# Causal attention stage: transposes and projections on half tiles of the array, in two phases per pair of row tiles

## The chip, the cores and the metric

The program runs on one core of one Trainium2 chip. A core has five engines with programs of their own: TensorE (PE, matmuls and transposes; its weight loads have rows of their own, PEld), VectorE (DVE), ScalarE (ACT), GpSimd (POOL) and SyncE (SP, which issues transfers here). They wait for each other by semaphores. The metric is the time of one execution in microseconds on the device, as a median of runs.

## The reference

Four layers, each an attention and a feed-forward part, on x of 2 x 1024 x 128 in float32. The change touches the attention of layer 2 alone, a causal one with 16 heads of 64:

```
latent_kv = x @ w_kv_down
kv = latent_kv @ w_kv_up
k, v = (kv[..., :HD], kv[..., HD:])
q = (x @ w_q).reshape(Bx, Tx, N_HEAD, HEAD_SIZE)
att = jnp.einsum('bqhd,bkhd->bhqk', q, k) * scale
att = jnp.where(causal, att, -jnp.inf)
att = jax.nn.softmax(att, axis=-1)
y = jnp.einsum('bhqk,bkhd->bqhd', att, v)
return y @ w_out
```

## The kernel before

`causal_stage` computes q, k, v, the scores, the softmax and the product with v, all in float32. Rows of the sequence are cut into 8 tiles of 128 for each of 2 batches, and heads go two at a time (`hp`, 8 steps), since two heads of 64 fill 128 partitions. Under the causal mask row tile `tb` has `tb + 1` blocks of 128 keys. The stage goes over 64 pairs `n`: 8 steps x 2 batches x 4 pairs, where a pair is a short row tile (j = 0 to 3, so 1 to 4 blocks) and a long one (7 - j, so 8 to 5 blocks). A pair always has 9 blocks for each of two heads.

The steps of a row tile are these. `score` multiplies q and k: K is 64 partitions, so the two heads stand in the upper and the lower 64 rows of the array, as tiles of 64 rows x 128 columns (the profile prints 64*128). DVE (`maximum`, L1887) adds the mask, writes the negated scores to `p` and keeps their minimum. ACT (`exponential`, L1838) takes the exponential in place and sums the row. `turn` (L1766) transposes each 128 x 128 block of `p` on PE against the identity, a 128*128 operation, up to four blocks into one PSUM bank. ACT or DVE copies that bank to `pT` (`move`, L1829 and L1876). `product` (L1780) multiplies v and `pT`; its weights are the 64 columns of one head of v, so the two heads stand in the left and the right half of the array, as tiles of 128 rows x 64 columns (128*64). At the end of a batch `take` (L1844) copies the sums from PSUM to `y`, `invert` (L1895) inverts the row sums on DVE, SP carries them through memory to all partitions, and POOL (L1924) multiplies `y` by them. `project` makes a piece of the next step's q or k (L1732, one matmul of 512 columns, 128*128) or v (L1737, four of 128 columns, 128*128); a step needs 12 pieces, and they are spread 2, 1, 2, 1 over the pairs. The last step has none.

A float32 matmul shows as two MATMUL and two LDWEIGHTS records, a transpose as one of each.

PE's order of one pair is: long scores, short transposes, product of the previous long tile, pieces, next short scores, long transposes of head 0, short product, long transposes of head 1. Transposes and pieces share PSUM banks 4 and 5 in turn (`groups`, `number`, `bank_of`). Each group has one mover, ACT or DVE, and `open_bank` lets PE write group g when group g - 2 has been copied. `settled` waits for the copies that a product or a score reads. Scores use banks 0 to 3, a head two of them, and wait until DVE has read the scores before (`max_done`).

The stage behind this one (`out_stage`, L1329) multiplies `y` by the output weights; its second half needs the last batch's `y` from POOL.

Of the kernel before, what the change touches and what calls it, by code (L numbers as in the profile page):

```python
# [1601 lines left out]
def causal_stage(nc, R, ctx, W, dram, lat, y):  # L1602
# [27 lines left out]
    PIECES = 12  # L1630
    PER_STEP = 8
# [10 lines left out]
    def parts_of(n):  # L1642
        return range(row_tile(n, 1) // 4 + 1)


    def short_turns(n):
        return [("turn", n, 0, (0, 1), 0)] if row_tile(n, 0) < 2 else [("turn", n, 0, (hh,), 0) for hh in range(2)]

    def long_turns(n, hh):
        return [("turn", n, 1, (hh,), part) for part in parts_of(n)]  # L1650

# [3 lines left out]

    def pieces(n):
        hp, j = n // PER_STEP, n % PER_STEP
        if hp + 1 == STEPS:
            return []
        first = 3 * (j // 2) + 2 * (j % 2)  # L1660
        return [(hp + 1, m) for m in range(first, first + (1 if j % 2 else 2))]


    groups = [(("project", 0, m), "da"[m % 2]) for m in range(PIECES)]
    for n in range(PAIRS):
        groups += [(x, "da"[i]) for i, x in enumerate(short_turns(n))]
        groups += [(("project", *x), "da"[i]) for i, x in enumerate(pieces(n))]
        groups += [(x, "ad"[i]) for i, x in enumerate(long_turns(n, 0))]
        groups += [(x, "da"[i]) for i, x in enumerate(long_turns(n, 1))]
    number = {what: g for g, (what, _m) in enumerate(groups)}  # L1670
    moved_by_a, moved_by_d = [0], [0]
    for _what, mover in groups:
        moved_by_a.append(moved_by_a[-1] + (mover == "a"))
        moved_by_d.append(moved_by_d[-1] + (mover == "d"))

    def bank_of(what):
        return 4 + number[what] % 2

# [34 lines left out]
    def on_pe(pe):  # L1713
        def settled(g):
            pe.wait_ge(t_a, moved_by_a[g + 1])
            pe.wait_ge(t_d, moved_by_d[g + 1])

        def open_bank(what):
            g = number[what]
            if g >= 2 and groups[g - 2][1] == "a":  # L1720
                pe.wait_ge(t_a, moved_by_a[g - 1])
            if g >= 2 and groups[g - 2][1] == "d":
                pe.wait_ge(t_d, moved_by_d[g - 1])
            return bank_of(what)

        def project(hp, m):
# [3 lines left out]
            if m < 8:  # L1730
                b, t = chunk(m % 4)
                pe.matmul(R.ps[:, bank, :], w[:, hp % 2, m // 4, :], h_chunk(R, m) if m < 4 else lat[:, b, t],  # L1732
# [8 lines left out]
        def score(n, long):  # L1741
# [8 lines left out]
            for c in range(end + 1):  # L1750
                cols = min(CW, full - c * CW)
                for hh in range(2):
# [3 lines left out]
                    if c == end:  # L1756
                        last.then_inc(s_full, 1)
# [904 lines left out]
```

## Time and profile before

| | us |
|---|---|
| median of 3 runs | 2167.46 |
| lowest and highest of them | 2165.61 and 2169.25 |
| the profiled execution's span, first to last instruction | 2163.0 |
| of it the causal stage, from its first piece to the last product | 562.4 |
| PE busy in the whole span | 2051.7 (95%) |
| DVE, ACT busy in the whole span | 1578.5, 1377.2 |

The page gives busy times by engine, a chain of work that ended last, and groups of instructions. A PE record lasts longer than its share of the array, because matmuls are pipelined: the distance from one stretch of equal instructions to the next tells what a stretch costs. "Idle before" is the time in which the engine had nothing running, with what ended it.

### The profile page before, as it was taken

To read this page: it belongs to the slowest core of one execution; us is meant where nothing else is said; L and a number is where in the kernel's file an instruction comes from. 1 tells how busy PE (TensorE), PEld (TensorE's weight loads), DVE (VectorE), ACT (ScalarE), POOL (GpSimd) and SP (SyncE) were. 2 spreads that over 40 slices of the span, in tenths; PEclk is the share of its full clock that TensorE was granted. 3 is DMA by queue.
4 is the path that set the end of the run, shared out by engine and by line. 5 is a ranking of instruction groups with operands and counts; after the bars stand their busy time and mean duration, and the time that the engine had idled before them with its cause. 6 is when DMAs were issued, how large, how long until landed. Compare 5 with 4: busy or idle time off the path is not lost. (4 is left out here: it accounts for less than half of the span.)

```text
span 2163.0 us, 40432 instructions
## 1 busy us (share of the span) xinstructions
PE 2051.7 (95%) x15666; PEld 901.1 (42%) x15666; DVE 1578.5 (73%) x2235; ACT 1377.2 (64%) x2731; POOL 208.9 (10%) x388
## 2 busy tenths in 40 slices
PE   7999999999999899999989999999999989999998
PEld 3222222222223422222336666666666434444453
DVE  7999999999984799999466565566655355555553
ACT  4899999999995389899755555555555322222253
POOL 3010111111023301111000000000000100000000
PEclk7999999999999799999999999999999999999999
DMA  3010100001000100110100111011101145554520
GB/s 97 4 26 15 32 21 24 21 25 28 15 25 10 40 22 22 27 38 12 29 5 11 22 17 25 11 25 15 21 11 22 26 95 119 128 122 115 121 60 20
DMA packets 107005, 82.44 MB, mean 38 GB/s; under 512 B 54720, under 2 KB 89536, under 8 KB 102864
## 3 DMA queue, kind: packets, MB, share of 16 engines
q1 hardware_dynamic: 105872, 79.05, 16.0%
q8 instruction: 120, 1.97, 0.4%
q10 hardware_dynamic: 432, 0.56, 0.1%
q0 software_dynamic: 528, 0.43, 0.1%
q14 instruction: 53, 0.43, 0.1%
HBM read 62.98 MB, written 2.42 MB: 30 GB/s over the span
## 5 line engine op out<-in xcount | busy, mean ns | idle before, releaser
L1069 DVE TENSOR_REDUCE a0nm<-ps 128x2 f32<-128x1024 f32 x512 | 586.4, 1213 | 10.4 <-PE ps L936 8.2
L1047 ACT ACTIVATE a0p<-ps 128x512 f32<-128x512 f32 x1024 | 544.2, 599 | 60.2 <-PE ps L956 43.5
L970 PE MATMUL ps<-a0p,a0vst 128*32 128x256 f32 x4096 | 328.0, 392 | 27.6 <-ACT a0p L1047 14.0
L1069 DVE TENSOR_REDUCE a1nm<-ps 128x2 f32<-128x1024 f32 x256 | 294.7, 1214 | 8.2 <-PE ps L936 7.3
L1047 ACT ACTIVATE a1p<-ps 128x512 f32<-128x512 f32 x512 | 275.6, 596 | 34.9 <-PE ps L956 26.0
L956 PE MATMUL ps<-a0qm,a0k 32*128 32x512 bf16 x1024 | 276.7, 387 | 0.0
L2120 ACT ACTIVATE ex_s<-ps 128x512 f32<-128x512 f32 x128 | 76.4, 597 | 252.9 <-PE ps L2075 252.9
L936 PE MATMUL ps<-a0k,a0q 32*128 32x512 bf16 x1024 | 202.9, 394 | 18.0 <-DVE a0nm L1069 15.8
L1887 DVE CUSTOM_DVE_ANT_0 cap_long<-ps,xc_res 128x1024 f32<-128x1024 f32 (+3 forms) x128 | 126.0, 1022 | 76.5 <-PE ps L1754 76.5
L1838 ACT ACTIVATE cap_long<-cap_long,canm 128x1024 f32<-128x1024 f32 (+3 forms) x128 | 125.3, 982 | 81.9 <-DVE canm L1887 81.9
L2209 DVE TENSOR_TENSOR ex_su<-ex_s,ps 128x512 f32<-128x512 f32 x128 | 88.1, 688 | 113.7 <-PE ps L2079 113.0
L970 PE MATMUL ps<-a1p,a1vst 128*32 128x256 f32 x2048 | 164.3, 393 | 6.4 <-ACT a1p L1047 5.5
L956 PEld LDWEIGHTS ps<-a0qm,a0k 32*128 32x128 bf16 x1024 | 79.2, 91 | 208.4 <-ACT a0p L1047 118.2
L1754 PE MATMUL ps<-cak,caq 64*128 64x512 f32 (+3 forms) x768 | 158.6, 517 | 2.3 <-DVE canm L1887 2.3
L936 PE MATMUL ps<-a1k,a1q 64*128 64x512 bf16 x512 | 149.9, 401 | 10.9 <-DMA a1q<-a1parts_sb 5.9
L956 PE MATMUL ps<-a1qm,a1k 64*128 64x512 bf16 x512 | 156.6, 386 | 0.0
L970 PEld LDWEIGHTS ps<-a0p,a0vst 128*32 128x32 f32 x4096 | 81.5, 108 | 155.8 <-ACT a0p L1047 70.7
L2075 PE MATMUL ps<-h_res,f2wg 128*128 128x512 f32 x256 | 130.7, 592 | 0.0
L2079 PE MATMUL ps<-h_res,f2wu 128*128 128x512 f32 x256 | 130.7, 592 | 0.0
L2063 PE MATMUL ps<-ex_hid,f2wd 128*128 128x512 f32 x256 | 130.5, 592 | 0.0
L1766 PE MATMUL ps<-ident_res,cap_long 128*128 128x128 f32 x832 | 122.4, 283 | 1.7 <-ACT capT_long L1829 0.9
L2220 DVE TENSOR_TENSOR ex_hid<-ex_su,ex_wb 128x512 f32<-128x512 f32 x128 | 88.6, 692 | 44.6 <-DMA ex_wb<-ex_w_dram 38.6
(324 smaller groups left out, 2531.6 us busy)
## 6 DMA issues: line engine op xcount, KB each, us to landing
ex_wb<-ex_w_dram SPq DMA_DIRECT2D x62, 512.0 KB, 6.2
carrow<-car_dram SPq DMA_DIRECT2D x32, 256.0 KB, 4.3
xc_res<-a0rec SPq DMA_DIRECT2D x15, 256.0 KB
a0q<-a0parts_sb SPq DMA_DIRECT2D x95, 32.0 KB, 2.0
a1q<-a1parts_sb SPq DMA_DIRECT2D x94, 32.0 KB
a0k<-a0parts_sb SPq DMA_DIRECT2D x90, 32.0 KB, 2.0
a1k<-a1parts_sb SPq DMA_DIRECT2D x84, 32.0 KB
f2wg<-in_ex_gate SPq DMA_DIRECT2D x32, 64.0 KB, 1.8
```

Source lines behind the costliest of these rows:

```text
L936: pe.matmul(R.ps[:, bank + d, :], q[rows, slot, rt, t0:t0 + 128], k[rows, slot, rt, hf * CW:(hf + 1) * CW], start=True, stop=True).then_in ...
L956: pe.matmul(R.ps[:, score_bank(n), :], k[rows, place(u)[3], rt, s * 128:(s + 1) * 128], qm[rows, u % 2, rt, :], start=True, stop=True).the ...
L970: last = pe.matmul(R.ps[32 * j:32 * j + 32, 6, cols], vst[:, g, s, j * HG // 4, :], p[:, s % 2, j, cols], start=(g == 0 and s == 0 and hal ...
L1047: act.activation(p[:, s % 2, e, :], R.ps[:, score_bank(n), :], ACT.Exp).then_inc(exp_done, 1)
L1069: dve.tensor_reduce(nm[:, u % 2, tb, 2 - 2 * z:4 - 2 * z, hf], R.ps[:, bank:bank + 2, :], X_AXIS, ALU.max, negate=True).then_inc(bank_free, 1)
L1754: last = pe.matmul(R.ps[:, 2 * hh + c, 0:cols], q[rows, hp % 2, b, tb * 128:(tb + 1) * 128], k[rows, hp % 2, b, c * CW:c * CW + cols], sta ...
L1766: last = pe.transpose(R.ps[:, bank, to:to + 128], p[long][:, hh, s * 128:(s + 1) * 128], R.ident[:])
L1838: act.activation(row, row, ACT.Exp, bias=nm[:, a % 4:a % 4 + 1], scale=-1.0, accum_out=rs[:, b, tb, hh:hh + 1]).then_inc(exp_done, 1)
L1887: dve.tensor_tensor_reduce(p[long][:, hh, 0:(tb + 1) * 128], src, late[:, T - (tb + 1) * 128:T], -1.0, LARGEST, ALU.add, ALU.min, nm[:, a ...
L2063: pe.matmul(R.ps[:, i % 4, :], wd[:, (i // 4) % 2, :], hid[:, i % 4, :], start=False, stop=True, skip_group_check=True).then_inc(d_done, 1)
L2075: pe.matmul(R.ps[:, G_BANK + 2 * (i % 2), :], wg[:, slot, :], h_chunk(R, c), start=True, stop=True)\
L2079: pe.matmul(R.ps[:, U_BANK + 2 * (i % 2), :], wu[:, slot, :], h_chunk(R, c), start=True, stop=True)\
```

## The change

Transposes: a 128 x 128 block of `p` is turned as two tiles, partitions 0 to 63 and 64 to 127, each 64 rows x 128 columns of the array with 64 moving columns. The upper rows go to one PSUM bank, the lower rows to the next one, so a `turn` now fills both banks 4 and 5; ACT copies the even group, DVE the odd one, each half of the columns. Eight blocks of a head fit in one turn (8 x 64 columns), so a long head is one turn of two groups, where it was two parts of up to four blocks.

Projections: each matmul is issued as two of 64 columns of the array (128*64), the left and the right half of the output's partitions, as the products are.

Order on PE: scores and transposes (all 64*128) come in one phase, products and pieces (all 128*64) in the other. The short scores of the next pair and the first bank of the next long scores are issued between the long transposes of this pair; short scores move to bank 1 or 3. The pieces are now two per pair for six pairs and none for two. ACT and DVE orders follow: exponentials and maxima are taken one head at a time, and `invert` stands behind the last copy of the batch.

```diff
+    HALVES = (slice(0, PH), slice(PH, 2 * PH))
...
+    def turns(n, heads, long):
+        return [("turn", n, long, heads, half) for half in range(2)]
...
+        if hp + 1 == STEPS or j >= PIECES // 2:
             return []
+        return [(hp + 1, 2 * j + i) for i in range(2)]
...
+        def open_bank(what):
+            g = number[what]
+            if g >= 2:
+                pe.wait_ge(t_d if g % 2 else t_a, moved(g - 2))
             return bank_of(what)
...
-                pe.matmul(R.ps[:, bank, :], w[:, hp % 2, m // 4, :], h_chunk(R, m) if m < 4 else lat[:, b, t],
-                          start=True, stop=True).then_inc(t_full, 1)
+                for cols in HALVES:
+                    last = pe.matmul(R.ps[cols, bank, :], w[:, hp % 2, m // 4, cols], h_chunk(R, m) if m < 4 else lat[:, b, t],
+                                     start=True, stop=True)
+                last.then_inc(t_full, 1)
...
+        def turn(pair):
+            _t, n, long, heads, _half = pair[0]
+            banks = [open_bank(what) for what in pair]
             pe.wait_ge(exp_done, scores_of(n, long) + heads[-1] + 1)
+            blocks = [(hh, s) for hh in heads for s in range(row_tile(n, long) + 1)]
+            for i, (hh, s) in enumerate(blocks):
+                for bank, rows in zip(banks, HALVES):
+                    last = pe.transpose(R.ps[:, bank, i * PH:(i + 1) * PH], p[long][rows, hh, s * 128:(s + 1) * 128],
+                                        R.ident[rows, rows])
+                    if i + 1 == len(blocks):
+                        last.then_inc(t_full, 1)
...
         for n in range(PAIRS):
-            score(n, 1)
-            for x in short_turns(n):
-                turn(x)
-            if n:
-                product(n - 1, 1)
-            for x in pieces(n):
-                project(*x)
             if n + 1 < PAIRS:
-                score(n + 1, 0)
-            for x in long_turns(n, 0):
-                turn(x)
-            product(n, 0)
-            for x in long_turns(n, 1):
-                turn(x)
-        product(PAIRS - 1, 1)
+                short_score(n + 1)
+            turn(long_turns(n, 0))
+            if n + 1 < PAIRS:
+                long_score_first(n + 1)
+            turn(long_turns(n, 1))
+            if n + 1 < PAIRS:
+                long_score_rest(n + 1)
+                turn(short_turns(n + 1))
+            product(n, 1)
+            if n + 1 < PAIRS:
+                for x in pieces(n + 1):
+                    project(*x)
+                product(n + 1, 0)
...
     def on_act(act):
...
         for n in range(PAIRS):
+            move(long_turns(n, 0)[0])
             if n + 1 < PAIRS:
+                exponential(n + 1, 0, 0)
+                exponential(n + 1, 0, 1)
+            move(long_turns(n, 1)[0])
+            if n + 1 < PAIRS:
+                move(short_turns(n + 1)[0])
+                exponential(n + 1, 1, 0)
+            if ends_batch(n):
+                take(n)
+            if n + 1 < PAIRS:
+                exponential(n + 1, 1, 1)
+                for x in pieces(n + 1)[0:1]:
+                    move(("project", *x))
...
     def on_dve(dve):
...
         for n in range(PAIRS):
             if n + 1 < PAIRS:
+                maximum(n + 1, 0, 0)
+            move(long_turns(n, 0)[1])
+            if n + 1 < PAIRS:
+                maximum(n + 1, 0, 1)
+            move(long_turns(n, 1)[1])
             if ends_batch(n):
                 invert(n)
+            if n + 1 < PAIRS:
+                maximum(n + 1, 1, 0)
+                move(short_turns(n + 1)[1])
+                maximum(n + 1, 1, 1)
+                for x in pieces(n + 1)[1:2]:
+                    move(("project", *x))
```

PE's queue before, from the long scores of the second pair of a batch (row tiles 1 and 6) to those of the next. Line L1754 are scores, L1766 transposes, L1780 products, L1737 pieces of v; `cap` is p, `capT` is pT, `cav` is v, and x counts matmuls of the program:

```order
L1754 MATMUL ps<-cak,caq 128x512 x2
L1754 MATMUL ps<-cak,caq 128x384 x2
L1766 MATMUL ps<-ident_res,cap_short 128x128 x4
L1780 MATMUL ps<-capT_long,cav 64x128 x16
L1737 MATMUL ps<-a2qkv,sq_res 128x128 x4
L1754 MATMUL ps<-cak,caq 128x384 x2
L1766 MATMUL ps<-ident_res,cap_long 128x128 x7
L1780 MATMUL ps<-capT_short,cav 64x128 x4
L1766 MATMUL ps<-ident_res,cap_long 128x128 x7
L1754 MATMUL ps<-cak,caq 128x512 x2
```

PE's queue in the changed kernel over the same work, from the short scores of row tile 1 to the short product of that pair (L1750 scores, L1777 transposes, L1792 products, L1741 pieces of v):

```order
L1750 MATMUL ps<-cak,caq 128x256 x2
L1777 MATMUL ps<-ident_res,cap_long 128x64 x16
L1750 MATMUL ps<-cak,caq 128x512 x2
L1777 MATMUL ps<-ident_res,cap_long 128x64 x16
L1750 MATMUL ps<-cak,caq 128x384 x2
L1777 MATMUL ps<-ident_res,cap_short 128x64 x8
L1792 MATMUL ps<-capT_long,cav 64x128 x16
L1741 MATMUL ps<-a2qkv,sq_res 64x128 x16
L1792 MATMUL ps<-capT_short,cav 64x128 x4
```

The shape of the tile changed at every row before; now the first six rows have one shape and the last three the other.

ACT's queue before, around the end of a batch: exponentials are L1838, copies of transposes L1829, the copy of the sums to y L1844, copies of pieces L1827:

```order
L1838 ACTIVATE cap_long,cars<-cap_long,canm 128x1024 x2
L1844 ACTIVATE y<-ps 128x512 x2
L1827 ACTIVATE cak<-ps 128x512
L1829 ACTIVATE capT_long<-ps 128x512
L1838 ACTIVATE cap_short,cars<-cap_short,canm 128x256 x2
L1829 ACTIVATE capT_long<-ps 128x512
```

ACT's queue in the changed kernel at the same place and through the pair behind it (exponentials L1852, copies of transposes L1844, the copy to y L1858, pieces L1842):

```order
L1852 ACTIVATE cap_long,cars<-cap_long,canm 128x1024
L1858 ACTIVATE y<-ps 128x512 x2
L1852 ACTIVATE cap_long,cars<-cap_long,canm 128x1024
L1842 ACTIVATE cav<-ps 128x512
L1844 ACTIVATE capT_long<-ps 128x8x64
L1852 ACTIVATE cap_short,cars<-cap_short,canm 128x256 x2
L1844 ACTIVATE capT_long<-ps 128x8x64
L1844 ACTIVATE capT_short<-ps 128x2x2x64
```

The copy to y now stands between the two long exponentials, and the copy of the second long head stands behind both short exponentials with the copy of the short transposes next to it.

## Rows read from the trace of the kernel before

**Rows 1.** The page: the chain that ended last, by engine, shares of the span.

```profile
PE 42%; ACT 3%; DVE 2%; issue 1%; DMA 1%; POOL 0%; POOLq 0%; SPq 0%; DVEq 0%
```

**Rows 2.** Windows: us, busy PE, PEld, DVE, ACT, POOL; clock, DMA share, GB/s.

```profile
1113.46:1675.86 562.40, 554.12 (x4609) 359.68 (x4609) 333.51 (x782) 312.54 (x736) 38.48 (x31) 1.00 0.11 18
200.00:600.00 400.00, 367.99 (x4140) 115.18 (x4136) 394.53 (x382) 365.00 (x710) 44.91 (x129) 1.00 0.09 23
```

**Rows 3.** Timeline of PE over one pair: start us, length us, engine, line.

```profile
1413.54 0.44 PE L1780 MATMUL ps<-capT_short,cav 128*64 128x128 f32 x4
1413.91 1.14 PE L1766 MATMUL ps<-ident_res,cap_long 128*128 128x128 f32 x8
1414.98 1.77 PE L1754 MATMUL ps<-cak,caq 64*128 64x512 f32 x8
1416.68 0.66 PE L1766 MATMUL ps<-ident_res,cap_short 128*128 128x128 f32 x4
1417.27 1.97 PE L1780 MATMUL ps<-capT_long,cav 128*64 128x128 f32 x32
1419.17 1.12 PE L1732 MATMUL ps<-h_res,a2qkv 128*128 128x512 f32 x2
1420.22 0.92 PE L1754 MATMUL ps<-cak,caq 64*128 64x384 f32 x4
1421.07 0.98 PE L1766 MATMUL ps<-ident_res,cap_long 128*128 128x128 f32 x7
1421.98 0.33 PE L1780 MATMUL ps<-capT_short,cav 128*64 128x128 f32 x2
```

**Rows 4.** The chain in order of time: start us, us, one piece of v.

```profile
1175.52 1.09 PE ps L1737 x8
```

**Rows 5.** Timeline of the experts' matmuls: lines change, the tile does not.

```profile
1800.83 1.02 PE L2063 MATMUL ps<-ex_hid,f2wd 128*128 128x512 f32 x2
1801.68 1.02 PE L2075 MATMUL ps<-h_res,f2wg 128*128 128x512 f32 x2
```

**Rows 6.** Timeline in narrow windows: weight loads of transposes and of scores; small transposes.

```profile
1377.37 0.20 PEld L1766 LDWEIGHTS ps<-ident_res,cap_long 128*128 128x128 f32 x2 [0.33 <-issue]
...
1376.74 0.19 PEld L1754 LDWEIGHTS ps<-cak,caq 64*128 64x128 f32 x2 [0.76 <-issue]
...
1376.74 0.30 PEld L1754 LDWEIGHTS ps<-cak,caq 64*128 64x128 f32 x4 [0.76 <-issue]
...
674.49 0.38 PE L1380 MATMUL ps<-ident_res,h_res 128*8 128x128 f32 x2
```

**Rows 7.** Groups by shape in the stage: count, busy us, mean ns of one.

```profile
L1766 PEld LDWEIGHTS ps<-ident_res,cap_long 128*128 128x128 f32 x832 | 88.5, 140 | 45.1 <-issue 26.2 <-ACT capT_long L1829 4.3 <-DVE caq L1874 3.8
...
L1829 ACT ACTIVATE capT_long<-ps 128x512 f32<-128x512 f32 x80 | 47.8, 598 | 69.8 <-PE ps L1766 69.3
...
L1838 ACT ACTIVATE cap_long<-cap_long,canm 128x1024 f32<-128x1024 f32 x32 | 36.7, 1147 | 46.2 <-DVE canm L1887 46.2
...
L1838 ACT ACTIVATE cap_short<-cap_short,canm 128x384 f32<-128x384 f32 x32 | 19.2, 605 | 0.0
```

**Rows 8.** Timeline: hand-overs from PE to DVE, and from DVE to PE.

```profile
1416.78 1.09 DVE L1887 CUSTOM_DVE_ANT_0 cap_long<-ps,xc_res 128x896 f32<-128x896 f32 x1 [1.49 <-PE ps L1754]
...
1375.21 0.42 DVE L1876 COPY capT_short<-ps 128x256 f32<-128x256 f32 x1
...
1375.68 0.30 PEld L1732 LDWEIGHTS ps<-sq_res,a2qkv 128*128 128x128 f32 x2 [0.96 <-DVE capT_short L1876]
```

**Rows 9.** Timeline of the end of the stage.

```profile
1672.37 0.24 DVE L1895 RECIPROCAL carinv<-cars 128x16 f32<-128x16 f32 x1
...
1674.62 1.31 PE L1780 MATMUL ps<-capT_long,cav 128*64 128x128 f32 x20 [0.77 <-DVE capT_long L1876]
1675.86 14.00 PE L1329 MATMUL ps<-y,a2wo 128*128 128x512 f32 x32
1690.32 0.70 PE L1329 MATMUL ps<-y,a2wo 128*128 128x512 f32 x1 [0.46 <-POOL y L1924]
```

More of the change, by code:

```diff
@@ L1736, in project @@
             for i in range(4):
-                last = pe.matmul(R.ps[:, bank, i * C:(i + 1) * C], lat[:, b, t.start + i * 128:t.start + (i + 1) * 128],
-                                 w[:, hp % 2, 2, :], start=True, stop=True)
+                for cols in HALVES:
+                    first = t.start + i * 128 + cols.start
+                    last = pe.matmul(R.ps[cols, bank, i * C:(i + 1) * C], lat[:, b, first:first + PH],
+                                     w[:, hp % 2, 2, :], start=True, stop=True)
@@ L1739, in project, with score_part @@
             last.then_inc(t_full, 1)
-        def score(n, long):
+        def score_part(n, long, c, bank, cols):
             hp, b, j = place(n)
             tb = row_tile(n, long)
-            if not long and n % PER_STEP == 0:
-                settled(number["project", hp, 7])
-            if scores_of(n, long):
-                pe.wait_ge(max_done, scores_of(n, long))
-            full = (tb + 1) * 128
-            end = tb // 4
-            for c in range(end + 1):
-                cols = min(CW, full - c * CW)
-                for hh in range(2):
-                    rows = slice(PH * hh, PH * hh + PH)
-                    last = pe.matmul(R.ps[:, 2 * hh + c, 0:cols], q[rows, hp % 2, b, tb * 128:(tb + 1) * 128],
-                                     k[rows, hp % 2, b, c * CW:c * CW + cols], start=True, stop=True)
-                    if c == end:
-                        last.then_inc(s_full, 1)
@@ L1759, in turn @@
-        def turn(what):
-            _t, n, long, heads, part = what
-            bank = open_bank(what)
-            pe.wait_ge(exp_done, scores_of(n, long) + heads[-1] + 1)
-            to = 0
-            for hh in heads:
-                for s in range(4 * part, min(4 * part + 4, row_tile(n, long) + 1)):
-                    last = pe.transpose(R.ps[:, bank, to:to + 128], p[long][:, hh, s * 128:(s + 1) * 128], R.ident[:])
-                    to += 128
-            last.then_inc(t_full, 1)
+            for hh in range(2):
+                rows = HALVES[hh]
+                last = pe.matmul(R.ps[:, 2 * hh + bank, 0:cols], q[rows, hp % 2, b, tb * 128:(tb + 1) * 128],
+                                 k[rows, hp % 2, b, c * CW:c * CW + cols], start=True, stop=True)
+                if not long or c:
+                    last.then_inc(s_full, 1)
```

155 lines of the change are left out of this document (73 added, 82 removed).

## The prediction, made before the changed kernel had run

> **What bounds the kernel now.** I read the chain that ended last first: PE has most of it [rows 1]. The change touches one stage, so I then read that stage's window: in its 562.4 us PE is busy 554.1, DVE 333.5, ACT 312.5, at a granted clock of 1.00 [rows 2]. PE sets the pace; the other two have some 40% of slack. What PE spends its time on is read from one pair [rows 3], as the distance from one stretch to the next.
>
> - Products: one block (x4) takes 0.37, eight (x32) take 1.90. So 0.218 us a block and 0.15 beside it.
> - Transposes: four take 0.59, seven take 0.91. So 0.109 each and 0.15 beside it.
> - Scores: three blocks take 0.85, seven take 1.70. So 0.213 a block (both heads at once) and 0.20 beside it.
> - A piece of q or k takes 1.05, one of v 1.09 [rows 4]: 0.855 and 0.89, and 0.20 beside it.
>
> What stands beside the work is paid once a stretch. Among the experts' matmuls, where the line changes but the tile stays 128*128, two matmuls follow two others 0.85 or 0.86 behind [rows 5]: nothing is paid. So it is paid where the tile's shape changes, which in this stage is at every stretch. Its parts: the first weight load cannot run ahead and shows in full (0.057 for a transpose, 0.053 for a product, 0.105 for 128 plain columns), and the rest, 0.094, is an empty array. The 0.057 is the gap between the first two weight loads of transposes: two end after 0.20, one lasts 0.140 [rows 6, 7]. The 0.105 is the same for scores: two heads end after 0.19, four loads after 0.30 [rows 6].
>
> **What the change removes.** The program has 502 shape changes before and 130 after.
>
> 1. Empty array: 372 x 0.094 = -35.0 us.
> 2. First loads that now hide under the matmul before: 128 scores x 0.105, 191 transposes x 0.057, 127 products x 0.053, 56 pieces x 0.105 make 36.9; after, 65 scores x 0.105 and 65 products x 0.053 make 10.3. So -26.6.
> 3. Transposes: 64 x 18 = 1152 blocks at 0.109. What is the 0.109? Transposes of 8 columns of weights and 128 moving ones have the same distance (x2 lasts 0.38, one 0.27 [rows 6]), so it is the moving side; 64 moving columns take 0.055. The load of the next half can start when the matmul before it starts and takes 0.057. Both halves at once, as the scores' two row halves do (two loads end after 0.19, one lasts 0.185), gives 0.057 to 0.060; I take 0.059. 1152 x 0.050 = -57.6. The bounds: 0.055 if the load hides wholly (-62), 0.080 if the four instructions per block press on each other (-33), and 0.109 and 0.218 below.
> 4. Pieces: the halves run side by side as the products' do, so 0.855 stays; v goes from 0.89 to 0.872, 32 times, -0.7.
>
> Together PE has 120 us less to do, which would leave 442 in the stage.
>
> **What it adds: waits.** Work that PE no longer has was cover. I laid the queues of PE, ACT and DVE end to end in program order, each step starting when its engine is free and its releaser is done, with these prices and three hand-overs: 0.19 from the array to DVE or ACT (seven score blocks of 0.213 from 1414.98, with 0.105 before them, end at 1416.58; DVE starts at 1416.78), 0.05 back (copy over at 1375.63, load at 1375.68) [rows 3, 8] and 0.05 between ACT and DVE. Exponentials and copies are as in [rows 7], shorter ones in proportion above a fixed 0.28 and 0.18. The same laying out of the kernel before gives 560.0 us, against 562.4 in the trace, with 17 us of waits. For the changed kernel it gives 501.5, with 74 us of waits. They stand in two places, and each can be followed.
>
> *Before the short transposes.* Both banks must be free, so ACT must have copied the even half of the second long head, and ACT does the two short exponentials first. With row tiles 2 and 5, from the end of that head's transposes: PE has 0.58 of scores left. ACT starts the second short exponential at 0.04 and ends it at 0.65 (0.605), copies 448 columns by 1.20 (0.55), PE can go at 1.31. Wait 0.7. With shorter short tiles it is 0.4, with the longest 1.0, and the last scores then wait 0.3 for DVE and a head's turn 0.1 to 0.2.
>
> *Behind the end of a batch.* ACT's queue is exponential, two copies to y, exponential, copy of a piece, and only then is bank 4 free for the next long head. From the end of the long scores: 0.2 + 1.2 of DVE (1.09 for 896 columns [rows 8], 1024 in proportion) + 0.05, then 1.15 + 1.06 + 1.15 + 0.60, so 5.5 with the hand-over. PE meanwhile has 0.2 + 0.15 + 1.1 + 1.7 + 0.2 + 0.2 + 0.4, about 4.2. Wait 1.3. In the last step there are no pieces, and the wait is 1.9 for PSUM of the products instead.
>
> Four pairs of a batch wait 0.2, 1.8, 1.0 and 1.6: 4.5 us, times 16 is 72, and 2 at the end. So: -120 + (74 - 17) = -63; the laying out has -58.5, since after a wait the first load shows again (up to 0.057 or 0.105 each time). I take -58.5.
>
> The page TensorEngine Tiling (Array Packing) of the Trainium skill, section PSUM Bottleneck, says the same in general: tiling makes TensorE faster, not the emptying of PSUM. That no run before shows, since its copies hide.
>
> **The end of the stage.** The inverse started at 1672.37, and the second half of the output stage at 1690.32, 17.95 later; its first half covers 14.0 of it from 1675.86 [rows 9]. The last product's array work ended about 1675.77, so the tail behind it was 14.55. Now `invert` stands behind the last two copies and starts about 1.2 before that end (3.4 before), so the tail is 16.7: +2.2.
>
> **Sum.** -58.5 + 2.2 = -56.3 on a span of 2163.0. The median is 4.5 above the profiled span, and nothing outside the stage changes, so 2167.5 - 56.3 = 2111.2. If each hand-over to PE costs 0.03 more, because a turn now waits for three semaphores, that is 2 more; with 0.080 a block 15 more; with 0.055 some 3 less. Own range 2100 to 2127.
>
> **Rivals.**
>
> *Transposes stay at 0.109 a block.* Either the loads run one behind another, two of 0.055, or PE issues no faster than the four instructions in 0.109 that the products show, the densest lasting stretch of the trace. Against it: scores load both halves at once. For it: nothing before has four in 0.06 for long. The laying out gives 541, so -19 + 2 = -17: 2150.5. TensorE: Matmul & The Clock Gate of the Trainium skill, section LDWEIGHTS, has a load take its columns over 1.2 GHz whatever the rows, 107 ns for 128 columns, which would be this case; the transposes' 0.057 speaks against it, the scores' 0.105 for it.
>
> *The halves run one behind the other, loads and matmuls.* A half then costs 0.109 as a whole block did, a block 0.218: 1152 x 0.159 more than I take, of which waits hide a little, laid out +97, so 2267. It is slower from 0.125 a block on, where the other gains are used up. Against it: the two heads of the scores and of the products do overlap, 0.213 and 0.218 for two. For it: no transpose in the trace is on a half. A clock that falls in the longer waits would act alike; the first attention keeps 1.00 with PE busy 92% of 400 us [rows 2].
>
> *Waits do not grow*, as copies and exponentials overlap better than laid out: -120 + 2, 2050.
>
> *The change does nothing to the price of a stretch*, because score and transpose differ in more than shape: 0.094 stays at, say, all stretches. Then 35 of the gain goes, and 2146. The small transposes [rows 6] follow and precede plain matmuls without a gap, which speaks against it.
>
> **How the numbers follow.** Forecast 0.74, transposes at 0.109 0.10, gap stays 0.04, waits do not grow 0.05, one behind the other 0.06, and 0.01 for no change. A range from 2098 to 2150 holds the forecast's case, the stretches' case and half of the first rival, about 0.83. A measurement can tell about 0.2% (4 us) from no change. Faster 0.93, same 0.01, slower 0.06.
>
> **What would show it.** In the trace after: transposes of 64 columns in pairs, a pair every 0.055 to 0.060; scores followed by transposes with no gap; a piece still 0.855; DVE and ACT busy as before within 5%; PE's waits on ACT's copies at the short transposes (0.4 to 1.0) and at the first long head behind a batch (1.3); the stage near 502; the inverse to the output's second half still near 18. I am wrong if a pair of transposes takes 0.1 or more, if the waits sum to under 50 or over 95, or if the clock in the stage is under 1.00.

## The result and the profile after

The changed kernel takes 2143.15 us in the median (2142.62 to 2149.75, 4 runs), the kernel before 2167.9 (2165.61 to 2169.25, 4 runs): a ratio of 0.9895, 95% interval 0.9881 to 0.9909. That is 24.8 us faster, where 56.3 were forecast. The spans are 2140.8 and 2163.0.

First the stage as one window, the answer to [rows 2]: us, then busy time of PE, weight loads, DVE, ACT and POOL, the granted clock, DMA share, GB/s.

```profile
1114.31:1647.84 533.53, 476.55 (x6145) 324.85 (x6145) 317.86 (x768) 336.95 (x782) 38.49 (x31) 0.97 0.11 19
```

The stage took 562.4 and takes 533.5. PE's busy time fell by 77.6, but PE is now idle for 57.0 us of the stage, and the clock is 0.97 where it was 1.00. DVE is busy for 4.7% less and ACT for 7.8% more, where both were forecast within 5%. The forecast had 501.5 for the stage.

The timeline of PE over the same pair as [rows 3] (row tiles 3 and 4) shows the new pattern.

```profile
1421.30 0.47 PE L1777 MATMUL ps<-ident_res,cap_long 64*128 64x64 f32 x10
1421.60 1.08 PE L1750 MATMUL ps<-cak,caq 64*128 64x512 f32 x4
1422.52 0.47 PE L1777 MATMUL ps<-ident_res,cap_long 64*128 64x64 f32 x10
1422.82 1.08 PE L1750 MATMUL ps<-cak,caq 64*128 64x512 f32 x4
1423.73 0.28 PE L1777 MATMUL ps<-ident_res,cap_short 64*128 64x64 f32 x4
1423.95 1.31 PE L1792 MATMUL ps<-capT_long,cav 128*64 128x128 f32 x20
1425.09 1.92 PE L1741 MATMUL ps<-a2qkv,sq_res 128*64 128x128 f32 x32
1427.07 0.44 PE L1792 MATMUL ps<-capT_short,cav 128*64 128x128 f32 x4
```

Five transposed blocks (x10) stand 0.30 ahead of the next scores, so 0.06 a block, with no room for the 0.15 that a change of shape cost in [rows 3]. The pieces of v (x32, 16 before) stand between products of their own shape. Over all blocks the distance of a pair of halves is 0.0625. So far all is as forecast.

What is not as forecast stands in one place of a step: the second long head of its fifth pair (j = 0 of the second batch), whose transposes end 7.9 us behind the start of the inverse of the first batch. From that pair's short product to the next one it is 10.4, 14.7, 12.8, 13.5, 14.8, 14.7 and 10.2 us in the first seven steps, and 9.1 in each of them in the first experiment below, which takes the cause away. The last step, which has no pieces, has no such excess. This is the timeline of ACT, DVE, PE and SP's queue in the second step. "<-DMA a0k" is a guess of the profile's: that transfer belongs to the first attention and is long over, so the name stands for "nothing that the records show".

```profile
1228.85 0.69 DVE L1892 COPY capT_long<-ps 128x512 f32<-128x512 f32 x1 [1.26 <-PE ps L1777]
...
1229.64 0.71 PE L1777 MATMUL ps<-ident_res,cap_long 64*128 64x64 f32 x16
...
1230.16 0.89 PE L1750 MATMUL ps<-cak,caq 64*128 64x384 f32 x4
...
1233.39 0.60 ACT L1844 ACTIVATE capT_long<-ps 128x512 f32<-128x512 f32 x1 [2.88 <-DMA a0k<-a0parts_sb]
1233.41 1.26 SPq L1703 DMA_DIRECT2D carrow<-car_dram  x2
1233.43 0.69 DVE L1892 COPY capT_long<-ps 128x512 f32<-128x512 f32 x1 [3.55 <-DMA a0k<-a0parts_sb]
```

PE's transposes of the second long head ended at 1230.3 and the scores behind them at 1231.05 or so. Both copies should have started at 1230.5. They start at 1233.4, both at once, and in the same 0.04 us SP's queue, which had waited for the store of the batch's inverses (L1697, 2048 pieces of 4 bytes), goes on to its loads. So the signals of PE, the copies' release, were **held** until about the store's last landing. The semaphore records in the trace say the same: the two halves of the transposes end at 1230.32 and 1230.35, their signals are recorded at 1233.37 and 1233.40, and the last recorded landing is at 1233.39. The same view of the kernel before, at such a landing (1240.24), has no hold: no copy in its stage starts more than 0.04 behind the recorded end of its transposes, if nothing else keeps its engine.

```profile
1238.15 1.36 PE L1766 MATMUL ps<-ident_res,cap_long 128*128 128x128 f32 x8
...
1238.84 0.60 ACT L1829 ACTIVATE capT_long<-ps 128x512 f32<-128x512 f32 x1
...
1239.55 0.69 DVE L1876 COPY capT_long<-ps 128x512 f32<-128x512 f32 x1 [0.52 <-PE ps L1766]
...
1240.24 1.26 SPq L1702 DMA_DIRECT2D carrow<-car_dram  x2
```

How often this occurs in the changed kernel's stage is in the table of waits (engine, line, releaser, us in total, times, longest). By it ACT's copies are held five times in long turns and once in a short one.

```profile
DVE capT_long L1892 <- DMA a0k<-a0parts_sb: 16.5, 5, 3.6
ACT capT_long L1844 <- DMA a0k<-a0parts_sb: 13.2, 5, 2.9
ACT capT_short L1844 <- DMA a0k<-a0parts_sb: 2.6, 1, 2.6
```

The table has only the waits to which the profile gives that name. By the copies' own rows, a copy is late by 0.8 to 3.1 us behind 11 of the 16 stores: in the place above in each of the first seven steps (1.2 to 3.1 us), and at a short turn behind four of the second batches (0.8 to 1.9).

A hold has a second price. Windows of 4 us around the one above:

```profile
1227.00:1231.00 4.00, 3.06 (x42) 1.63 (x40) 1.46 (x5) 2.70 (x8) 0.00 (x0) 1.00 0.02 2
1231.00:1235.00 4.00, 0.83 (x12) 0.69 (x12) 1.57 (x2) 0.68 (x2) 0.00 (x0) 0.74 0.00 0
1235.00:1239.00 4.00, 4.00 (x40) 4.00 (x42) 1.47 (x5) 2.45 (x5) 0.00 (x0) 0.50 0.64 137
1239.00:1243.00 4.00, 4.00 (x58) 3.27 (x54) 1.45 (x4) 0.92 (x2) 2.50 (x2) 0.91 0.00 1
```

PE was idle for most of 1231 to 1235, and behind that its granted clock is 0.50, the lower of its two levels (1.2 in place of 2.4 GHz). There eight blocks of products (x32) take nearly twice the 1.90 of [rows 3]:

```profile
1234.84 3.68 PE L1792 MATMUL ps<-capT_long,cav 128*64 128x128 f32 x32
```

Last, the tail, the answer to [rows 9]:

```profile
1646.29 0.24 DVE L1914 RECIPROCAL carinv<-cars 128x16 f32<-128x16 f32 x1
...
1647.77 14.00 PE L1329 MATMUL ps<-y,a2wo 128*128 128x512 f32 x32
...
1657.51 1.26 SPq L1703 DMA_DIRECT2D carrow<-car_dram  x2
...
1665.06 8.83 PE L1329 MATMUL ps<-y,a2wo 128*128 128x512 f32 x16 [3.29 <-POOL y L1949]
```

From the stage's last products to the output's second half it is 17.3 now and was 14.5. Behind the 3.3 us in which PE waits, 16 matmuls take 8.83 where half of the 32 before take 7.0: the lower clock again.

### The profile page after: what moved, and what is told of

The parts are those of the page before. It is cut to its first block and busy times, and to the rows that moved or that the text cites. A ratio compares the mean times of both kernels' runs of the same rounds, so it can differ in the third digit from the quotient of the medians.

```text
span 2140.8 us, 43376 instructions
## 1 busy us (share of the span) xinstructions
PE 1976.6 (92%) x17202; PEld 867.0 (41%) x17202; DVE 1562.8 (73%) x2221; ACT 1401.6 (65%) x2777; POOL 208.7 (10%) x388
## 5 line engine op out<-in xcount | busy, mean ns | idle before, releaser
L1069 DVE TENSOR_REDUCE a0nm<-ps 128x2 f32<-128x1024 f32 x512 | 586.9, 1216 | 10.4 <-PE ps L936 8.2
L1750 PE MATMUL ps<-cak,caq 64*128 64x512 f32 (+3 forms) x768 | 172.2, 524 | 0.0
L1852 ACT ACTIVATE cap_long<-cap_long,canm 128x1024 f32<-128x1024 f32 (+3 forms) x128 | 126.3, 986 | 22.3 <-DVE canm L1906 18.3
L1844 ACT ACTIVATE capT_long<-ps 128x512 f32<-128x512 f32 (+3 forms) x128 | 65.4, 511 | 97.9 <-PE ps L1777 84.6
```

Of the source, the lines that this page charges most:

```text
L1069: dve.tensor_reduce(nm[:, u % 2, tb, 2 - 2 * z:4 - 2 * z, hf], R.ps[:, bank:bank + 2, :], X_AXIS, ALU.max, negate=True).then_inc(bank_free, 1)
L1750: last = pe.matmul(R.ps[:, 2 * hh + bank, 0:cols], q[rows, hp % 2, b, tb * 128:(tb + 1) * 128], k[rows, hp % 2, b, c * CW:c * CW + cols], ...
L1852: act.activation(row, row, ACT.Exp, bias=nm[:, a % 4:a % 4 + 1], scale=-1.0, accum_out=rs[:, b, tb, hh:hh + 1]).then_inc(exp_done, 1)
```

## The experiments

Theory S says that the small pieces of the store cause the loss, by holding PE's signals, and by the lower clock that follows. In the runs that store by rows, and in the one that stores pairs, the inverses come back in another order, so that y is scaled by the wrong ones; the work is otherwise the same.

### The store by rows, in the changed kernel

```diff
-sp.dma_start(r_dram[b].rearrange("a q -> q a"), rinv[:, b]...)      # 2048 pieces of 4 bytes
+sp.dma_start(r_dram[b]... viewed as 128 rows of 16, rinv[:, b]...)  # 128 rows of 64 bytes
```

> The changed kernel, with the store of the 2048 inverses of a batch as 128 rows of 64 bytes in place of 2048 pieces of 4 bytes; they come back in another order, so this run's numbers are scaled by the wrong rows. Theory S (the store): in the changed kernel PE's signals of the pair after a batch arrive up to 3.1 us late, each time at the moment at which the store's last pieces land; the idle time then halves the granted clock for 3.4 or 6.8 us. Without the small pieces no signal is late, no window of the stage has a clock under 1.00, and the stage is what the laying out gives with 0.0625 a transposed pair, 503.5 (measured with the store: 533.5). The tail behind it gets 3 us shorter as well, since the output's first half hides a shorter store: 2143 - 30 - 3 = 2110, 2105 to 2116. Rival Q (the queues): the late signals belong to how PE, ACT and DVE wait for one another there, and the landing only falls beside them. Then the stage stays at 533 and only the tail shrinks: 2140, 2137 to 2144.

Measured: 2109.74 (2107.39 to 2111.16), ratio 0.9739 (0.9722 to 0.9755). The stage:

```profile
1113.05:1618.08 505.03, 465.29 (x6144) 314.53 (x6144) 317.94 (x768) 336.28 (x782) 38.49 (x31) 0.99 0.09 20
```

It is 505.0, and the table of waits has no row of the kind above. No copy is late any more. Theory S holds and Q falls. The two prices can be read off as well. Against the changed kernel PE is busy for 11.3 us less (476.55 - 465.29), which is the lower clock, and idle for 17.2 us less (56.98 - 39.74), which is the holds. Two short spells at the lower clock are left in the last step, where no pieces fill the waits.

### The inverse first

```diff
+if ends_batch(n): invert(n)        # at the head of the pair
 maximum(n + 1, 0, 0); move(long_turns(n, 0)[1]); maximum(n + 1, 0, 1); move(long_turns(n, 1)[1])
-if ends_batch(n): invert(n)
```

> The changed kernel, with the inverse of a batch (and with it the store) put before the two copies of long transposes rather than behind them, some 5 us earlier in the pair. Theory S: the landings come some 5 us earlier, where PE, ACT and DVE are at the same pair's short transposes or products; signals are then late there, and how much it costs depends on which waits are near: the stage 505 to 530, and no late signal at the old place (the scores and long transposes that end 10 us behind the store's issue). Rival Q: the place of the pair makes it, so the late signals stay where they were and the stage stays at 533. Under both the tail is 3 us shorter, for the inverse starts earlier against the last product: 2140 with Q, 2112 to 2137 with S.

Measured: 2117.04 (2116.37 to 2119.98), ratio 0.9769 (0.9753 to 0.9785), the stage 515.5. The table has three holds left, and shorter ones:

```profile
ACT capT_long L1844 <- DMA a0k<-a0parts_sb: 7.4, 3, 2.7
```

The tail gains too. I had expected no late signal at the old place, and that was wrong: the same copies are late in each of the first seven steps, by 0.8 to 2.0 us. Their transposes now end 9.0 us behind the start of the inverse, 7.9 before, so the store was only 1.1 us earlier against them, and not the 5 that I had taken. With a landing 1.1 us earlier the holds shrink, which theory S has and Q has not.

### The store made twice

```diff
+for d in (r_dram, r_dram2):
     sp.dma_start(d[b]..., rinv[:, b]...).then_inc(r_out, 16)
```

> The changed kernel, with the store of the inverses made twice, the second time to a place that nobody reads; the loads wait for both. Theory S: twice as many small pieces land, over twice the time, so the signals are late by twice as much or are late twice: 16 stalls of 1 to 3 us more, and longer spells at half the clock, the stage 550 to 590, the whole 2170 to 2210 with some 8 us of a longer tail. Rival Q: the stage stays at 533, and only the tail grows, by the 8 to 10 us of the second store, less the 1 us that PE waits for nothing there: 2152.

Measured, one execution: 2186.05, the stage 568.6, inside what S gave. ACT's held copies of this kind go from 13.2 us in 5 to 26.3 in 9.

```profile
ACT capT_long L1846 <- DMA a0k<-a0parts_sb: 26.3, 9, 4.4
```

### One signal in place of two

```diff
-                    if i + 1 == len(blocks):
-                        last.then_inc(t_full, 1)
+            last.then_inc(t_full, 2)
```

> The changed kernel, with one signal (an increment by two) at the last transpose of a pair of halves in place of two increments 31 ns apart. If two increments of one semaphore so close to each other are what gets stuck (rival B, the burst), the late signals go and the stage is near 504, the whole 2113. With theory S or Q nothing changes but 0.03 us at each copy on ACT: 2143, 2139 to 2147.

Measured, one execution: 2129.77, the stage 519.8, between the two. Neither expectation held. By the table five holds remain, but shorter ones, so a burst of two increments is not the cause; fewer signals do shorten the holds.

```profile
ACT capT_long L1843 <- DMA a0k<-a0parts_sb: 9.3, 5, 2.2
```

### The kernel before, by rows and twice

The same two edits in the kernel before.

> The kernel before, with the store of the inverses as 128 rows of 64 bytes (they come back in another order, so its numbers are scaled by the wrong rows). The trace of before has every signal of PE within 0.02 us of its instruction's end while the small pieces land. If the small pieces cost only in the changed kernel (theory S), the stage stays at 562.4, the tail loses the 0.46 us that PE waits there before the output's second half, and the whole is 2166.9, 2165 to 2168. Then the changed kernel without small pieces is 57 us ahead of this one, with the predicted terms alone. If the small pieces cost before too, unseen (rival G, a general cost), the stage is shorter here as well, by up to 10 us: 2157.

> The kernel before, with the store of 2048 small pieces made twice. In the changed kernel that lengthened the stage by 35 us, from 533.5 to 568.6. If any signal of PE can be caught by the landings (rival G), and the kernel before only has none at the wrong moment, then landings that last 8 us in place of 2 catch some here: the stage grows by 10 to 40 us, 2185 to 2215 with the tail. If it takes the changed kernel's half transposes (theory S, as narrowed), the stage stays at 562 to 564 and only the tail grows, by the 10 to 12 us of the second store behind the first: 2178, 2174 to 2182.

Measured by rows: 2166.68, ratio 0.9997 (0.9987 to 1.0007). Stored twice, one execution: 2180.44. The stage by rows, and stored twice:

```profile
1116.56:1678.66 562.10, 553.80 (x4608) 359.52 (x4608) 333.47 (x782) 312.55 (x736) 38.45 (x31) 1.00 0.08 18
```

```profile
1114.15:1678.23 564.08, 554.05 (x4609) 359.50 (x4609) 333.29 (x782) 312.17 (x736) 38.39 (x31) 1.00 0.18 18
```

So the small pieces cost the kernel before nothing in the stage (562.1 and 562.4), and 2 us when doubled. But doubled, they hold signals here too, behind two of the 16 batches, with whole transposes and the old order: by 2.1 us in these rows, and by 1.1 at 1663.1.

```profile
1632.97 0.69 DVE L1878 COPY capT_long<-ps 128x512 f32<-128x512 f32 x1 [2.95 <-DMA a0k<-a0parts_sb]
1633.02 0.49 ACT L1831 ACTIVATE capT_long<-ps 128x384 f32<-128x384 f32 x1 [2.13 <-DMA a0k<-a0parts_sb]
1633.24 1.27 SPq L1704 DMA_DIRECT2D carrow<-car_dram  x2
```

Without the small pieces the two kernels are 562.1 - 505.0 = 57.1 apart in the stage, where the forecast had 58.5. What remained open was what in the changed kernel lets a signal be held so often with a single store.

### Each part of the change undone, with the store by rows

Whole transposes, first by a matmul with 64 columns of the identity:

```diff
-last = pe.transpose(R.ps[:, bank, ...], p[long][rows, hh, ...], R.ident[rows, rows])
+last = pe.matmul(R.ps[:, bank, ...], p[long][:, hh, ...], R.ident[:, rows], start=True, stop=True)
```

> The changed kernel with the store by rows, and with its 64-column transposes made on the whole array (all 128 rows of weights, the same 64 columns out, the same banks, copies and order; the result of a transpose is the same). This takes out the tiling of the transposes alone: the two halves of a block run one behind the other, 0.11 a block in place of 0.0625, and each turn is a change of tile shape again. The laying out with 0.109 gives a stage of 562.6 in place of 503.5, so +59 on the 2109.7 of the tiled one: 2169, 2160 to 2178. If the loads of 128 rows by 128 columns show in full beside the matmuls (rival L, 0.055 + 0.057 for each half, 0.22 a block), the stage is near 690, the whole 2290. If it is below 2150, the shape changes cost less than the trace of before made me take.

Measured: 2550.55, ratio 1.1771 (1.1751 to 1.179). The chain has 2.82 us for six blocks, 0.47 a block.

```profile
1401.31 2.82 PE ps L1777 x24
```

The row counts 24 matmuls where the code has 12 for the six blocks. So a float32 matmul is made of two, and a float32 transpose of one. The expectation of 2169 missed by far, but the run says nothing on the tiling, since it changed the kind of instruction too. The next one has true transposes of whole blocks:

```diff
+for half, bank in enumerate(banks):
+    for i, (hh, s) in enumerate(blocks_of(n, long, heads, half)):   # blocks 0-3 | 4-7, or head 0 | head 1
+        last = pe.transpose(R.ps[:, bank, i * 128:(i + 1) * 128], p[long][:, hh, ...], R.ident[:])
+    last.then_inc(t_full, 1)
```

> The changed kernel with the store by rows, and with transposes of whole 128 by 128 blocks on the whole array, true transposes as in the kernel before: the first four blocks of a long head go to one bank and the rest to the other, of a short row tile one head to each. This undoes the tiling of the transposes and keeps the new order and the two-column-tile pieces. Laid out with 0.109 a block, and each turn a change of tile shape again, the stage is 561.0 in place of 503.5, so +57.5 on 2109.7: 2167, 2160 to 2172. If the changes of shape do not cost at turns what the trace of before showed, it is down to 2140.

Measured: 2166.09, ratio 0.9996 (0.9987 to 1.0006); the stage:

```profile
1116.14:1678.70 562.56, 542.11 (x4992) 350.66 (x4992) 310.33 (x768) 348.24 (x782) 38.45 (x31) 1.00 0.08 18
```

Tiling the transposes, with the changes of shape that it saves, is worth 57.5 us in the stage, to 0.1 what the laying out gave. With whole transposes, the new order and the split pieces are worth nothing: 562.6 against 562.1 of the kernel before.

The pieces whole:

```diff
-for cols in HALVES: last = pe.matmul(R.ps[cols, bank, :], w[:, hp % 2, m // 4, cols], ...)
+last = pe.matmul(R.ps[:, bank, :], w[:, hp % 2, m // 4, :], ...)      # v alike
```

> The changed kernel with the store by rows, and with the projections' pieces on the whole array (128 by 128), as before; transposes stay as two row tiles. Each pair with pieces has two changes of tile shape more, and their first loads show: the laying out gives 513.9 in place of 503.5, so +10.4 on 2109.7: 2120, 2117 to 2123. If splitting the pieces gains nothing, because the halves' loads or the product beside them cost what the change of shape saves, it is 2110.

Measured: 2120.03, ratio 0.9783 (0.9767 to 0.98), the stage 515.24. So 10.2 us for the pieces, where the laying out gave 10.4.

### What lets a signal be held

The last two kernels again, with whole transposes and with whole pieces, now with the store in small pieces:

> The same kernel with the store in small pieces of 4 bytes, as in both kernels. If it takes the half transposes for a signal to be held (theory H), its stage is that of its sister with the store by rows within 3 us, as was so for the kernel before (562.1 with rows, 562.4 with pieces), and no signal of PE is late: some 2168. If it is the changed kernel's order of the work that puts PE's signals in the landings' way (theory O), the signals are late here too, by 1 to 3 us in the fifth pair of each step, and the stage is 10 to 30 us longer than its sister's: 2180 to 2200.

> The changed kernel with the small pieces of the store kept and the projections' pieces on the whole array; its sister with the store by rows has a stage of 515.2. Theory H or O: signals are held as in the changed kernel, and the stage is 530 to 545, the whole 2140 to 2155. If it is the half loads of the projections (rival P) that make the signals be held, none is late here, the stage is 515 to 518 and the whole 2122 to 2126.

Measured, one execution each: whole transposes 2172.76, the stage 563.2 (562.6 by rows); whole pieces 2126.29, the stage 516.35 (515.24 by rows). The first has one copy that is late, by 0.65 us; it fits theory H and speaks against the order (theory O). The second I had not expected: the half transposes and the order are those of the changed kernel, and yet nearly all the loss is gone. So the halves of the *pieces* matter. These are the windows of 8 us from a batch's inverse on: changed kernel behind a first batch; changed kernel behind a second; whole pieces; whole transposes; the kernel before.

```profile
1222.45:1230.45 8.00, 7.00 (x106) 5.24 (x104) 4.97 (x13) 5.72 (x13) 0.00 (x0) 1.00 0.14 4
1257.57:1265.57 8.00, 6.97 (x82) 4.00 (x80) 5.03 (x14) 5.72 (x14) 0.00 (x0) 1.00 0.13 3
```

```profile
1227.64:1235.64 8.00, 7.17 (x90) 5.33 (x88) 5.03 (x14) 5.72 (x14) 0.00 (x0) 1.00 0.13 2
```

```profile
1235.00:1243.00 8.00, 7.06 (x78) 4.71 (x74) 4.82 (x12) 5.47 (x12) 0.00 (x0) 1.00 0.13 2
```

```profile
1230.27:1238.27 8.00, 7.87 (x60) 4.04 (x55) 4.32 (x10) 4.63 (x13) 0.00 (x0) 1.00 0.12 1
```

Busy times are alike; the matmuls are 106, 82, 90, 78 and 60. The long holds stand with the 106: two pieces of v, which the change made of 32 matmuls in place of 16, lie in that stretch. The count is not all: with one signal in place of two it is 106 as well, with holds up to 2.3, and with the inverse first 104, with holds up to 2.0. Theory D: a dense PE and the store's pieces together make the hold. Two more runs test its two sides.

```diff
-return [(hp + 1, 2 * j + i) for i in range(2)]
+return [(hp + 1, m) for m in ((0, 1), (2, 3), (8, 9), (10, 11), (4, 5), (6, 7))[j]]   # q, v, k
...
-sp.wait_ge(t_full, number["project", hp - 2, PIECES - 1] + 1)                         # SP's weight loads
+sp.wait_ge(t_full, number["project", hp - 2, 7 if hp > 2 else 11] + 1)                # wait for the last piece
```

> The changed kernel with the small pieces of the store kept, and the projections' pieces in another order: q, v, k in place of q, k, v. So the pair behind the first batch of a step has two pieces of k (8 matmuls in the trace) where it had two of v (32 matmuls). Nothing else changes; the laying out gives 503.8 for either order. Theory D (density): a signal is held when PE sends many instructions in the 8 us between the inverse and the landings: 106 matmuls there with holds of 2.3 to 3.1 us, 90 with holds up to 0.8 (pieces whole), 82 with holds of 0 to 1.9, 78 with 0 in most (whole transposes), 60 with none (the kernel before). Here it is 82 behind both batches: holds of 0 to 1.9, few or no spells at half the clock, the stage 507 to 520 in place of 533.5, the whole 2117 to 2130. Theory H (it takes half transposes and nothing else, which are unchanged): the stage stays at 530 to 535, the whole 2140 to 2145.

```diff
-sp.dma_start(r_dram[b].rearrange("a q -> q a"), ...)     # 2048 pieces of 4 bytes
+sp.dma_start(r_dram[b]... viewed as q t h, rinv[:, b])    # 1024 pieces of 8 bytes
```

> The changed kernel with the store of a batch as 1024 pieces of 8 bytes in place of 2048 of 4 (the inverses come back in another order, so the numbers are scaled by the wrong rows). If a hold needs both a dense PE and a backlog of small pieces, half the pieces land 4 to 5 us behind the inverse, before most of the dense stretch is over, and few signals are held: the stage 504 to 512, the whole 2110 to 2118. If any store of small pieces holds signals as long as PE is dense, it is 520 to 535, and 2127 to 2142.

Measured: the other order of pieces 2113.59 (2112.37 to 2113.95), ratio 0.9751 (0.9734 to 0.9767); half as many small pieces 2112.12, one execution, the stage 506.9, the store landed 4.3 us behind the inverse (1224.43 to 1228.76). The stage with the other order, and its 8 us:

```profile
1115.38:1620.98 505.60, 465.40 (x6145) 313.83 (x6145) 318.34 (x768) 335.49 (x782) 38.53 (x31) 1.00 0.12 20
...
1223.81:1231.81 8.00, 6.97 (x82) 3.99 (x80) 5.03 (x14) 5.72 (x14) 0.00 (x0) 1.00 0.13 2
```

With the 2048 pieces, the half transposes and the order of engines untouched, exchanging v and k takes 27.9 us out of the stage. In both orders the transposes of the place above end 7.9 us behind the inverse, and the last landing comes 10 to 12 us behind it; what differs is the matmuls ahead. The copies of that place are on time now (within 0.1 us), and those of a short turn are late behind six stores, by 0.6 to 1.3. That is theory D, and H falls. In the changed kernel, taking away either the dense stretch or half of the pieces is enough. Neither is a sharp condition: the kernel before had its two holds with twice the pieces and 77 and 78 matmuls in the 8 us ahead. And the run in pairs does not tell the number of pieces from their time, since its store had landed (4.3 us behind the inverse) before the transposes in question ended (7.9).

### A version without small pieces

```diff
+if ends_batch(n): invert(n)        # at the head of the pair, as in the second experiment
...
+pe.transpose(R.ps[0:16, bank, CW - PH:CW], rinv[rows, b]..., R.ident[rows, rows])   # for each half, its bank
+act / dve: copy of its half, 16x64, to rT
-sp.dma_start(r_dram[b].rearrange("a q -> q a"), rinv[:, b]...)
+sp.dma_start(r_dram[b], rT[:, b, :])                                                 # 16 rows of 512 bytes
```

> A kernel with the right output and without the small pieces: the changed kernel, but the inverse is made at the start of the pair, PE turns it in two more halves at the head of the second long head's transposes (128 by 16 to 16 by 128), ACT and DVE copy one half each (16 by 64), and the store is 16 rows of 512 bytes. With theory S no signal is late: the stage is that of the run with the store by rows, 505, plus at most 0.25 us a batch for the small copy on ACT before the short transposes' copy, so 505 to 509, and the tail is 14 as there: 2112, 2108 to 2116. If the signals are held for another reason that lives in the store's time and not its pieces, the stage is 515 to 533 and the whole 2120 to 2140.

Measured: 2109.97 (2107.28 to 2111.86, 5 runs), ratio 0.9734 (0.9721 to 0.9747). It beats both kernels, by 57 and 33 us.

```profile
1116.16:1621.02 504.86, 466.08 (x6176) 313.37 (x6177) 320.55 (x784) 338.40 (x798) 38.55 (x31) 1.00 0.09 20
```

```profile
1619.82 0.31 SPq L1700 DMA_DIRECT2D car_dram<-carT  x1
1621.02 20.87 PE L1329 MATMUL ps<-y,a2wo 128*128 128x512 f32 x48
...
1621.19 1.89 SPq L1705 DMA_DIRECT2D carrow<-car_dram  x2
```

The stage is 504.9, where the inverse at the head alone gave 515.5. No copy is late. The last store lands 1.4 us behind its issue, where the one in small pieces took 11.0 (1646.56 to 1657.51), and the output's 48 matmuls run through without a gap. The 16 small copies on each engine cost nothing that can be seen: the stage is that of the store by rows (505.0).

## Why the prediction was wrong, point by point

- *Direction and mechanism*: right. PE bound the stage, and less to do there made it shorter.
- *Empty array and hidden first loads*: borne out as a sum. They can't be told from the transposes' own price, but the two together came out: undone for the transposes 57.5 (laid out 57.5), for the pieces 10.2 (10.4).
- *Transposes at 0.059 a block*: 0.0625, which the laying out turns into 503.5 in place of 501.5. The rivals of 0.109, and of halves one behind the other, were wrong.
- *Waits*: the places were right, and the sizes near. Behind a batch the first long head waits for ACT's copy of a piece ("L1777 ... [0.94 <-ACT cav L1842]", with 0.25 ahead of it that the row's modelled end hides, so 1.2; forecast 1.3). Two sums in the prediction are slightly off: PE's terms there add up to 3.95 and not to about 4.2, which would make the wait 1.5, and the four waits of a batch to 4.6 and not to 4.5. The 74 us of waits can't be read off directly: PE's idle time is 57.0 in the stage, and 39.7 with the store by rows, but the modelled ends hide part of each wait, as above. What can be compared is the stage: 503.5 laid out with 0.0625, and 505.0 measured by rows, 504.9 with the turned inverse.
- **The step that failed** is the hand-over, "0.19 from the array to DVE or ACT", which the laying out took for every signal. In the held ones it is up to 3.1, and the clock that falls behind it was put at 1.00, where the stage had 0.97, which the prediction had named as a sign of being wrong. Together that is 28.5 of the stage (533.5 against 505.0): 17.2 of idle time and 11.3 of slower work. No term of the sum was for this, and no row of before showed it, since there the same store costs nothing.
- *The clause on the clock*: "a clock that falls in the longer waits would act alike", weighed against the first attention at 92% busy. Without the holds, the waits that were forecast (up to 1.9 us) left two spells of 3.4 us at the lower clock in the stage; with them there are six spells, 30.7 us in all, five of them behind holds of 2.3 to 3.1 us.
- *Tail*: forecast 16.7 from the last array work, measured 17.3 from the output's start. That was about right, but the 3.3 us of PE's wait in it brought 1.8 us of lower clock that was not in the sum.
- In sum: -58.5 became -28.9 in the stage, and +2.2 became +2.8 and 1.8, which makes -24.3. The spans are 22.2 apart and the medians 24.8; the 2 us between lie outside the stage and the tail, within what executions of one kernel differ by. Own range, 2100 to 2127, did not hold the time. The wider one, 2098 to 2150, did, by luck of its width: "gap stays" and "transposes at 0.109" give times close to 2143, and neither happened.

## What to carry to other kernels

A transfer of thousands of tiny pieces may cost nothing today and much tomorrow: when a change makes an engine issue twice the instructions in the same time, look at what lands in its densest stretch, and give such a transfer long rows first (here two more small transposes and two small copies a batch). When two engines restart at the same moment behind an engine that had long finished, ask what else ended at that moment. Waits that are laid out by hand can be right to 1.5 us in a stage of 505 and still miss a cost that only appears between parts, so compare pair by pair: the excess here stood in one pair of eight, and that found it.

## What the runs showed of the hardware

- PE's signals can arrive up to 3.1 us behind the end of their instruction, while a store of 2048 pieces of 4 bytes is about to land and PE sends its matmuls densely (106 in 8 us, each with a weight load). With the density of the kernel before (60 in 8 us) a single such store held none; two at once held signals by 2.1 and 1.1 us (77 and 78 in 8 us). With 1024 pieces of 8 bytes none was held. In the pair shown the signals came with the last landing, in another 0.9 us ahead of it (copies at 1300.63, SP's loads at 1301.56), so it is not the last landing itself that frees them. Which part of the chip holds them stays open. At the hold shown only 8 of the store's 16 landings have a record in the trace, and at every landing of the kernel before all 16 (one hold of 2.3 us has all 16 too). A full path of records might do this, which no run here tested. The Trainium skill, NOTIFIC — the notification-queue block, section Overflow: three behaviours, one of which stalls the engine, says that the block's inner pipeline holds back the one that produces records rather than losing any. The late signals would fit that rule, the missing records do not; and behind the fourteenth store 8 of 16 are missing and no copy is late. Every execution measured here was recorded, so whether an unrecorded one has the holds was not tried.
- A store of 2048 4-byte pieces takes 11.0 us from its issue to its landing (1646.56 to 1657.51); 16 rows of 512 bytes take 1.4. DMA: Bandwidth & Descriptors of the Trainium skill, section Rules for kernel authors, says that a strided last dimension becomes one descriptor an element. The trace agrees: from 1114 to 1690 the changed kernel has 34416 packets under 512 bytes and the run in pairs 18032, so 1024 more for each of 16 stores.
- A float32 matmul of 64 columns is two matmuls in the trace, each with its own load of the weights. On the whole array two of them, so four records, take 0.47 on one block, where the true transpose of a block takes 0.109. As an estimate, the loads set this: 0.12 a record, near the 0.105 that [rows 6] gave for a load of 128 columns.
